# First attention: the maxima's score matmuls of both heads given out in one step, steps spread over the units

## The reference

```python
qkv = (x @ qkv_w + qkv_b).reshape(Bw, Nw, 3, nh, dh)
attn = jnp.einsum('bnhd,bmhd->bhnm', q * scale, k)
attn = jax.nn.softmax(attn + bias[None], axis=-1)
out = jnp.einsum('bhnm,bmhd->bnhd', attn, v).reshape(Bw, Nw, Cd)
return out @ proj_w + proj_b
```

## Time and profile before

| | |
|---|---|
| runs | 2576.27, 2593.48 and 2595.0 us, median 2593.48 |
| profiled execution | 2582.66 us, its span 2580.9 us |
| mean granted clock of TensorE | 0.901 of full speed |
| busy share of the span | TensorE 90%, VectorE 71%, ScalarE 55%, GpSimd 16% |
| first attention, prologue | from 334.7 to 370.4 us of the span |
| first attention, 32 pairs | from 370.4 to about 1223 us, 26.60 us a pair where nothing disturbs it |

### The profile page before, as it was taken

How to read it: one execution, slowest core, us unless ns; L and a number is a source line. 1 busy time by engine, 2 the same in 40 slices (tenths; PEclk the granted TensorE clock), 3 DMA queues, 4 the chain that set the end, 5 groups by cost and what they waited for, 6 DMA issues and landing times.

```text
span 2580.9 us, 55201 instructions
## 1 busy us (share of the span) xinstructions
PE 2334.8 (90%) x20147; PEld 1072.7 (42%) x20178; DVE 1837.4 (71%) x4732; ACT 1422.1 (55%) x2576; POOL 424.9 (16%) x502
## 2 busy tenths in 40 slices
PE   8987679999999999999689998987799999699998
PEld 3326523333333333332544444576544444533333
DVE  4566768888888888884367776659767775366775
ACT  2116727777777777777045553327666667144443
POOL 2002200000000000000623332132100110411110
PEclk9997769999999999999589997655699999589999
DMA  3113620101101010030755552245612222734422
GB/s 96 25 31 102 219 66 26 39 26 36 29 26 39 26 38 27 26 65 6 164 148 154 158 146 61 65 116 155 239 45 67 69 93 44 160 75 100 97 61 60
DMA packets 254351, 208.23 MB, mean 81 GB/s; under 512 B 191571, under 2 KB 197892, under 8 KB 253828
## 3 DMA queue, kind: packets, MB, share of 16 engines
q1 hardware_dynamic: 240914, 176.43, 25.8%
q0 software_dynamic: 10368, 19.06, 2.6%
q10 hardware_dynamic: 2808, 9.22, 1.5%
HBM read 138.78 MB, written 65.90 MB: 79 GB/s over the span
## 4 chain that ended last, share of the span: by engine, by line
PE 75%; DVE 10%; ACT 5%; issue 4%; POOL 3%; DMA 2%; SPq 1%; DVEq 0%; ACTq 0%; POOLq 0%
PE ps L1580 11%; PE ps L1486 7%; PE ps L1551 6%; PE ps L2813 3%; PE ps L2293 3%; PE ps L2800 3%; PE ps L2309 3%; PE ps L1191 3%; PE ps L1165 3%; PE ps L2824 3%; PE ps L364 3%; PE ps L1576 3%; PE ps L376 2%; PE ps L1103 2%; PE ps L1106 1%
## 5 line engine op out<-in xcount | busy, mean ns | idle before, releaser
L1666 DVE TENSOR_REDUCE att_mpart<-ps 128x1 f32<-128x512 f32 x1024 | 633.9, 684 | 56.3 <-PE ps L1486 51.2
L1624 ACT ACTIVATE att_p<-ps 128x704 f32<-128x704 f32 x768 | 546.5, 760 | 215.5 <-PE ps L1551 208.3
L1580 PE MATMUL ps<-att_p,att_v 128*9 128x352 f32 x3072 | 301.3, 463 | 0.1
L1486 PE MATMUL ps<-att_kT,att_qT 64*128 64x512 bf16 x1024 | 281.2, 386 | 21.0 <-DMA att_qz<-qt_d 8.4
L1551 PE MATMUL ps<-att_qT,att_kT 64*128 64x352 bf16 x1536 | 251.5, 317 | 7.3 <-ACT att_p L1624 6.9
L1280 DVE TENSOR_REDUCE cau_mpart<-ps 128x1 f32<-128x512 f32 (+5 forms) x384 | 193.1, 552 | 81.1 <-PE ps L1106 67.9
L1247 ACT ACTIVATE cau_p<-ps 128x704 f32<-128x704 f32 (+6 forms) x272 | 171.6, 660 | 82.3 <-PE ps L1165 49.7
L1457 POOL DMA_DIRECT2D o_d<-att_o x128 | 64.3, 509 | 840.7 <-ACT att_o L1607 840.5
L1551 PEld LDWEIGHTS ps<-att_qT,att_kT 64*128 64x128 bf16 x1536 | 82.0, 93 | 273.5 <-issue 263.9
L2367 ACT ACTIVATE mo_g<-ps 128x768 f32<-128x768 f32 x176 | 133.2, 807 | 105.3 <-PE ps L2293 105.3
L2881 ACT ACTIVATE mo_act<-ps 128x512 f32<-128x512 f32 (+1 forms) x216 | 109.7, 559 | 145.2 <-PE ps L2800 145.1
(11 more groups left out here) (412 smaller groups left out, 3894.8 us busy)
## 6 DMA issues: line engine op xcount, KB each, us to landing
mo_gate<-wg_d SPq DMA_DIRECT2D x176, 192.0 KB, 4.1
mo_gate<-wg_d SPq DMA_DIRECT2D x64, 256.0 KB, 5.2
qt_d<-pre_qT SPq DMA_DIRECT2D x8, 1056.0 KB, 4.3
kt_d<-pre_kT SPq DMA_DIRECT2D x8, 1056.0 KB, 7.2
att_kT<-kt_d SPq DMA_DIRECT2D x32, 264.0 KB, 2.8
att_qT<-qt_d SPq DMA_DIRECT2D x32, 264.0 KB, 3.0
cqt_d<-cpr_qT SPq DMA_DIRECT2D x8, 1056.0 KB, 4.4
cau_qT<-cqt_d SPq DMA_DIRECT2D x16, 528.0 KB, 4.0
```

The lines of the kernel that those rows point to most:

```text
L1486: mm = pe.matmul(ps[:, bank, :], qT[half(s), u, j * P:(j + 1) * P], kT[half(s), u, c * BANK:(c + 1) * BANK], start=True, stop=not near)
L1580: mm = pe.matmul(ps[32 * cg:32 * cg + DV, 7, 0:TH], v[:, u, i, s, :], p[:, r, s, :], start=i < 2, stop=i == FULL - 1)
L1624: e = act.activation(p[:, n % PRING, :, :], ps[:, bank:bank + 2, 0:TH], ACT.Exp)
L1666: red = dve.tensor_reduce(mpart[:, j, s, c:c + 1], ps[:, bank, :], AX.X, ALU.max)
```

## The change

The numbers of the side work become `AHEAD, BETWEEN = 10, 4`, so the list `side` still has 39 entries, each stretch of maxima begins with head 0, and maxima 2 and 3 (the ones with corrections) stand together ahead of the turns. The entries are then joined to steps: two full maxima of one query tile and key half, the two for the last keys, and the two turns make one step each; the three for the last queries stay single. That gives 21 steps, and `cut` spreads these 21 over the 27 units. Six units (0, 4, 9, 13, 18 and 22) have none, the others one.

A step of two waits with `ring_free` for both of its banks before its first matmul. For two full maxima the matmuls of head 0 and head 1 then follow each other, and behind both the corrections where there are any. For the last keys the matmuls of the two heads alternate, and the corrections follow in one block. The prologue gives out its first 10 maxima one at a time.

```diff
-    AHEAD, BETWEEN = 9, 3
+    AHEAD, BETWEEN = 10, 4
...
-    cut = [len(side) * c // NU for c in range(NU + 1)]
+
+
+    def mates(x, y):
+        if "turn" in (x[0], y[0]):
+            return x[0] == y[0]
+        first, then = maxes[x[2]], maxes[y[2]]
+        return first[0] == then[0] and (then[1] == 1)
+
+
+    steps = []
+    for pos in range(len(side)):
+        if steps and len(steps[-1]) == 1 and mates(side[steps[-1][0]], side[pos]):
+            steps[-1].append(pos)
+        else:
+            steps.append([pos])
+    cut = [len(steps) * c // NU for c in range(NU + 1)]
...
-            def max_scores(m, u):
+            def max_scores(ms, u):
...
+                    for m, s, bank in heads:
+                        mm = pe.matmul(ps[:, bank, :], qT[half(s), u, j * P:(j + 1) * P], kT[half(s), u, c * BANK:(c + 1) * BANK],
+                                       start=True, stop=not near)
+                        if not near:
+                            mm.then_inc(mx_mm, 1)
                     if near:
+                        for m, s, bank in heads:
+                            for x in range(3):
+                                mm = pe.matmul(ps[:, bank, 384:512], eye[:, :], cor[:, 2 * u + s, x, 0:P], start=False, stop=x == 2)
+                            mm.then_inc(mx_mm, 1)
+                elif kind == "keys":
+                    for t in (*range(1, FULL), 0):
+                        for m, s, bank in heads:
+                            pe.matmul(ps[:, bank, t * TT:(t + 1) * TT], qT[half(s), u, t * P:(t + 1) * P], kT[half(s), u, TX:N],
+                                      start=True, stop=t > 0)
...
-                ring_free(pos, k, last)
+                for pos in step:
+                    ring_free(pos, k, last)
                 if kind == "max":
-                    max_scores(n, slot)
+                    max_scores([side[pos][2] for pos in step], slot)
                 else:
-                    turn(n, slot, pos)
+                    for pos in step:
+                        turn(side[pos][2], slot, pos)
```

More of the change, by code:

```diff
@@ L1324, in attend_heads @@
     third_last = [5 * t + 4 for t in range(3)]
-    maxes = [("full", s, j, c) for j in range(FULL) for c in range(2) for s in range(2)]
-    maxes += [("keys", s, 0, 0) for s in range(2)] + [("query", 0, 0, c) for c in range(3)]
+    full = [("full", s, j, c) for j in range(FULL) for c in range(2) for s in range(2)]
+    keys = [("keys", s, 0, 0) for s in range(2)]
+    query = [("query", 0, 0, c) for c in range(3)]
+    maxes = full + keys + query
     NM = len(maxes)
-    AHEAD, BETWEEN = 9, 3
+    AHEAD, BETWEEN = 10, 4
     side = ([("max", 1, m) for m in range(AHEAD, NM)] + [("max", 2, m) for m in range(BETWEEN)]
@@ L1478, in ring_free @@
                 apart(pe, const)
-            def max_scores(m, u):
-                kind, s, j, c = maxes[m]
-                bank = 4 + place[m]
+            def max_scores(ms, u):
+                kind, _, j, c = maxes[ms[0]]
+                heads = [(m, maxes[m][1], 4 + place[m]) for m in ms]
                 if kind == "full":
                     near = j == 0 and c == 1
-                    mm = pe.matmul(ps[:, bank, :], qT[half(s), u, j * P:(j + 1) * P], kT[half(s), u, c * BANK:(c + 1) * BANK],
-                                   start=True, stop=not near)
-                    if near:
-                        for x in range(3):
[L1490 to L1497, removed]
-                else:
-                    mm = pe.matmul(ps[0:2 * TT, bank, 0:TH], qz[:, u, :], kT[:, u, c * TH:(c + 1) * TH], start=True, stop=True)
-                mm.then_inc(mx_mm, 1)
@@ new lines, in max_scores @@
+                    for m, s, bank in heads:
[3 more added lines that the diff above has]
+                            mm.then_inc(mx_mm, 1)
+                    if near:
+                        for m, s, bank in heads:
[7 more added lines that the diff above has]
+                                      start=True, stop=t > 0)
+                    for m, s, bank in heads:
+                        for x in range(3):
+                            mm = pe.matmul(ps[:, bank, 0:TT], eye[:, :], cor[:, 2 * u + s, x, P:160], start=False, stop=x == 2)
+                        mm.then_inc(mx_mm, 1)
+                else:
+                    for m, _, bank in heads:
+                        c = maxes[m][3]
+                        pe.matmul(ps[0:2 * TT, bank, 0:TH], qz[:, u, :], kT[:, u, c * TH:(c + 1) * TH], start=True, stop=True)\
+                            .then_inc(mx_mm, 1)
@@ L1511, in turn, with side_step @@
                 mm.then_inc(t_mm, 1)
-            def side_step(it, u, pos, last):
-                kind, ahead, n = side[pos]
+            def side_step(it, u, step, last):
+                kind, ahead, n = side[step[0]]
                 if last and u + ahead >= U:
@@ L1532, in _ @@
                     pe.wait_ge(mx_red, m)
-                max_scores(m, 0)
-            for pos in range(len(side)):
-                side_step(-1, U - 1, pos, False)
+                max_scores([m], 0)
+            for step in steps:
+                side_step(-1, U - 1, step, False)
             def scores(it, u, g, last):
@@ L1559, in scores @@
                     mm.then_inc(s_mm, 1)
-                    for pos in range(cut[first_unit[g] + c], cut[first_unit[g] + c + 1]):
-                        side_step(it, u, pos, last)
+                    for s in range(cut[first_unit[g] + c], cut[first_unit[g] + c + 1]):
+                        side_step(it, u, steps[s], last)
             def values(it, u, g):
```

## The result

The changed kernel is slower: 2639.98 us median (2629.5 to 2643.11) against 2585.48 us for the kernel before on the same chip, a ratio of 1.0203 with a 95% interval of 1.0147 to 1.026. I had forecast +37 us; the medians are 54.5 us apart, and 2.03% of 2585.48 is 52. The profiled execution took 2641.4 us, 58.8 more than that of before.

A forecast was written before the change was run, and what follows sets the result against it. It took VectorE's 23.88 us of work plus ring-of-three-banks gaps to bound a pair; 30 pairs x 1.1 = 33 us plus 4 us prologue gave +37 us, 2620 or 2630 us by base, named 2625 us, range 2578 to 2652.

The forecast's parts named there:

- the size of nearly every gap: VectorE's waits in a pair, at key unit, queries and turns: 3.9 us forecast against 2.7 before.
- the 0.2 us left at the keys: At the last keys' maxima, VectorE's gap of 0.77 us would mostly go, leaving 0.2 us.
- two reductions stand behind the chain where I had said one: In VectorE's order after L1713, the changed profile should show one reduction, then a gap.
- The price of a joined step to VectorE: Each step of two in the three-bank ring costs VectorE 0.04 us, or some 0.1 where other work comes between.
- The term that decides: Units 20 to 26: unit 21's step waits for maximum 0's bank behind VectorE's chain; +1.4 us a pair.
- VectorE's work plus its gaps: Steady pairs: length is VectorE's 23.88 us of work plus its gaps, 3.9 against 2.7 us; +1.2 us a pair.
- TensorE was the true bound: Rival: lone matmuls' time comes back, a pair could reach 25.6 us, total 2562 us; chance 0.13.
- Gain and loss cancel: Rival: evener spread of units 0 to 17 fills more gaps, -0.1 to +0.6 us a pair, about 2600 us; chance 0.22.
- The wait spreads: Rival: unit 21's wait delays PV and ScalarE's exponentials, a pair loses up to 2 us, 2650 us; chance 0.1.
- the walk: Step-by-step timing of one pair: +1.4 us in units 20 to 26 less 0.35 before, +1.05 us a pair.
- The prologue, +4 forecast: Prologue at granted clock 0.50: joined steps leave VectorE 0.26 us idle about 16 times, one lone maximum +0.8; +4 us taken.
- such a drop: Steady pairs: a fall of the granted clock from 1.00 would make the prediction wrong; no term held it.

The follow-up runs named there:

- experiment 3: Changed kernel with a second att_mpart buffer and VectorE's chain moved behind maximum 1 of the pair after; 2636.92 us, ratio 1.0203 to the kernel before.
- experiment 4: Changed kernel with maxima 2 and 3 not joined, its 22 steps spread anew over the 27 units; 2638.46 us, ratio 1.0204 to the kernel before.
- experiment 6: Changed kernel with its joined steps placed by a table instead of the even spread; 2607.83 us, ratio 1.0081 to the kernel before.
- Experiment 5: Changed kernel with nothing joined, each single entry in the unit where the changed kernel has it; 2627.18 us, ratio 1.0168 to the kernel before.
- experiment 1: Changed kernel with its numbers 10 and 4 but nothing joined, 39 single entries spread over 27 units; 2579.28 us, ratio 0.9983 to the kernel before.
- experiment 2: Changed kernel, but in a step of two full maxima the second bank is waited for only behind head 0's matmul; 2624.81 us, ratio 1.0139.
- Experiment 7: Kernel before with VectorE's full reductions halved to 256 of 512 columns; 2547.83 us, ratio 0.9852 to the kernel before.
- experiment 8: Changed kernel with VectorE's full reductions halved to 256 of 512 columns; 2590.25 us, ratio 1.0017 to the kernel before.
- experiment 9: Changed kernel with nothing joined, numbers 11 and 4, single entries in units chosen by hand; 2556.37 us, ratio 0.9892 to the kernel before.
- experiment 10: The same kernel as experiment 9, in a second, longer set of runs; 2555.94 us, ratio 0.9892 to the kernel before.

## Why the prediction was right, and where it was not

**What held.** That the change would be slower, that the joined steps take TensorE's busy time down and don't shorten the pair, and the size of nearly every gap: 0.3, 0.6, 0.9, 0.3, 0.5 and 0.3 us forecast, 0.31, 0.54, 0.86, 0.25, 0.55 and 0.36 measured. Only the 0.2 us left at the keys didn't come, and two reductions stand behind the chain where I had said one. The price of a joined step to VectorE, 0.04 to 0.1 us, shows in the runs of reductions: 0.02 to 0.03 us for each, two to a step.

**The term that decides** held as well, and in its place. The step of unit 21 goes out 1.97 us after the start of unit 20 (884.56 to 886.53), where I had 1.96 (659.71 to 661.67). Units 20 to 26 lost 1.52 us, where I had 1.4. My experiment 3 seemed to refute this, but it only changed what the step and the turns behind it wait for; in experiments 4 and 6, in which the wait is gone or nearly so, units 20 to 26 take 7.85 and 7.81 us in place of 8.99. Both edits move other entries too, so about 1.1 us is the most that the wait alone cost.

**What the prediction had wrong** is why these waits are there. It put them on the joining, because a step of two needs two free banks. Experiment 5 against 1 shows that the units of the entries decide, 1.47 us a pair with nothing joined. Joining them then gives 0.12 us back (experiment 5 to 2, 27.79 to 27.67), and waiting for both banks up front takes 0.28 (27.67 to 27.95). The even spread of 21 steps counts a query maximum (0.52 us of VectorE) like a joined pair of full ones (1.28 us), leaves six units empty and puts up to four joined steps in a row. Then the second entry of a unit needs the bank of the first entry of the unit just before, one round trip of 1.25 us. It also puts the last query in unit 19 and maximum 0 in unit 20. The four runs that have this with both of maxima 2 and 3 in unit 21 take 8.8 to 9.1 us for units 20 to 26 (the changed kernel, experiments 2, 3 and 5); the three that have the query and maximum 0 earlier take 7.8 (experiments 1, 4 and 6). The kernel before has them where the changed one has, but only maximum 2 in unit 21, and that doesn't need the bank of maximum 0: 7.47 us.

**VectorE's work plus its gaps** as the length of a pair holds of necessity, and it gave a good number. Experiment 7 bears it out for the kernel before. For the changed order experiment 8 refutes it as a cause: with 8.2 us less of work on VectorE the loss against the old order is as large as ever.

**The rivals.** "TensorE was the true bound" is refuted: its busy time fell to 24.85 us, and the pair grew. "Gain and loss cancel" didn't come. "The wait spreads" wasn't seen: ScalarE is busy for 19.31 us of a pair before and 19.05 after, and most of what it waits for in the pair are scores.

**The terms that were too small.** The profiled executions are 58.8 us apart and not 37. In the pair the walk gave +1.05 and it is +1.35: 0.2 us because the first two thirds didn't come out even, as I had assumed (17.60 us against 17.39), and 0.12 in units 20 to 26, where the step with its six corrections takes 0.76 us (886.53 to PV at 887.29) in place of 0.64. With the first pair and the last but one that is 42 us in place of 33. The prologue, +4 forecast, is +6.2:

```profile
352.01 0.61 PE L1504 MATMUL ps<-att_kT,att_qT 64*128 64x512 bf16 x2 [1.04 <-DVE att_mpart L1694]
353.47 0.61 PE L1504 MATMUL ps<-att_kT,att_qT 64*128 64x512 bf16 x2 [0.85 <-DVE att_mpart L1694]
```

The 0.26 us a joined step hold (1.46 us from step to step in place of 1.20). With the maximum that goes out alone they make 3.5 us up to the start of the chain; the other 2.7 us come behind it, around the turns, at the lower clock. The pairs at the lower granted clock, about 6 us, had no term; I had named such a drop as what would make the prediction wrong. The spread of the pairs (1.5), the later start (1.8) and the rest of the program (1.4) had none either. So the named 2625 us was 15 us short of the median, with the loss of a pair put at 1.1 us where it is 1.35; the stated range was wide enough to hold what had no term.

That the clock falls because TensorE stands isn't shown. Runs with up to four joined steps in a row have such stretches (experiments 2, 3 and 4 one, one and two of them), those of 1, 5, 6, 7, 8, 9 and 10 none behind the first pair; but in the run of 8 the order is that of the changed kernel, and the ordinary pair's stretch shown above has the same busy time as the one ahead of a fall.

## What to carry to other kernels

Where TensorE feeds VectorE through a ring of few banks, count the round trip (matmul, reduction, two hand-overs) against the distance of an entry to the entry whose bank it needs; giving out two tiles at once in a ring of three brings that distance down to the tiles just given out. Spread side work by what it costs its consumer, not by the number of its steps: with the same instructions, the units and the number `AHEAD` alone moved this kernel from 1.7% slower to 1.1% faster. Where a short chain on one engine stands between two steps of another, start the chain earlier or put other work between, as experiments 4 and 6 did, so that the second step doesn't stand for it. And read an experiment by stretches, not by its total: experiment 4 took a wait away, won 1.14 us where it had stood and lost 1.22 elsewhere, because its edit moved other entries too, and the total looked as if the wait had cost nothing.

## What the runs showed of the hardware that was not expected

The granted clock fell to its lower level in four pairs of the changed kernel. In the one read TensorE was busy for 5.71 of the 6.80 us ahead and never idle for more than about 1.1 us; such a stretch cost a pair 1.5 us. The same stretch of an ordinary pair, with the same 5.71 us, wasn't followed by a fall, so no run here tells what decides it.

The two hand-overs were the same wherever I read them at the full clock: 0.03 to 0.04 us from the shown end of a matmul to the reduction that waits for it, 0.14 to 0.15 us from the end of a reduction to the matmul that needs its bank. In the prologue, where each maximum is given out alone behind the reduction of the one before, the second is 0.06 us (336.84 + 0.69 to 337.59 in the earlier trace rows); why it is shorter there stays open.
